# First attention of a two-layer gated block: one quarter of the heads takes its exponential straight from PSUM on ScalarE

## The reference

```python
HEADS = 16; HEAD_DIM = EMBED // HEADS; EXP_DIM = 2 * HEAD_DIM
def _feature_map(x, fm_w, fm_b):
    z = jnp.einsum('nshd,ed->nshe', x, fm_w) + fm_b
    return jnp.concatenate([jnp.exp(z), jnp.exp(-z)], axis=-1)
v, k, q = (_feature_map(x, fm_w, fm_b) for x in (v, k, q))
scores = jnp.einsum('nqhd,nkhd->nhqk', q, k) / jnp.sqrt(jnp.float32(EMBED))
attn = jax.nn.softmax(scores, axis=-1)
out = jnp.einsum('nhql,nlhd->nqhd', attn, v)
return out.reshape(N, S, HEADS * EXP_DIM) @ fc_w.T + fc_b
```

## Time and profile before

| what | value |
|---|---|
| median of 3 runs | 2163.36 us (2162.54 to 2164.04) |
| the profiled execution | 2158.57 us, of it 2156.8 us span |
| TensorE busy | 2027.2 us (94%) |
| VectorE busy | 1896.5 us (88%) |
| ScalarE busy | 1579.3 us (73%) |
| GpSimd busy | 1571.2 us (73%) |

### The profile page before, as it was taken

How to read it: one execution, slowest core, us unless ns; L and a number is a source line. 1 busy time by engine, 2 the same in 40 slices (tenths; PEclk the granted TensorE clock), 3 DMA queues, 4 the chain that set the end, 5 groups by cost and what they waited for, 6 DMA issues and landing times. The chain is left out here.

```text
span 2156.8 us, 82951 instructions
## 1 busy us (share of the span) xinstructions
PE 2027.2 (94%) x28378; PEld 1574.6 (73%) x28380; DVE 1896.5 (88%) x4324; ACT 1579.3 (73%) x3515; POOL 1571.2 (73%) x1456
## 2 busy tenths in 40 slices
PE   3999999977999999999999699999999966999999
PEld 2788888854666666666666689999999954777776
DVE  6899999987888888888888689999999968888888
ACT  3788888866555555655565678888888856888887
POOL 1576777742666666666666789999999943888888
PEclk9999999987999999999999899999999988999999
DMA  5100000002422223222221355555555530000000
GB/s 172 24 6 6 6 7 6 7 2 59 112 84 88 78 82 89 80 79 89 81 78 34 60 82 83 91 83 91 83 90 84 82 73 1 15 10 15 10 15 15
DMA packets 476587, 121.41 MB, mean 56 GB/s; under 512 B 431895, under 2 KB 446871, under 8 KB 475876
## 3 DMA queue, kind: packets, MB, share of 16 engines
q1 hardware_dynamic: 475140, 120.38, 25.4%
q10 hardware_dynamic: 1376, 0.10, 0.0%
HBM read 106.51 MB, written 13.89 MB: 56 GB/s over the span
## 5 line engine op out<-in xcount | busy, mean ns | idle before, releaser
L1286 POOL TENSOR_TENSOR f_low<-f_hidden,f_high 128x512 f16<-128x512 f32 x336 | 442.5, 1322 | 218.2 <-ACT f_high L1218 216.3
L1244 DVE TENSOR_TENSOR f_hidden<-f_hidden,f_share 128x512 f32<-128x512 f32 x336 | 372.8, 1110 | 0.0
L1434 POOL TENSOR_TENSOR f_low<-f_hidden,f_high 128x512 f16<-128x512 f32 x256 | 296.4, 1159 | 68.3 <-ACT f_high L1377 65.2
L1224 ACT ACTIVATE f_act_out<-f_gate 128x512 f32<-128x512 f32 x336 | 200.4, 596 | 193.3 <-PE f_gate L1188 193.1
L1267 DVE SCALAR_TENSOR_TENSOR f_hidden<-f_up,f_act_out 128x512 f32<-128x512 f32 x336 | 229.7, 684 | 82.5 <-PE f_up L1188 52.3
L1218 ACT ACTIVATE f_high<-f_hidden 128x512 f16<-128x512 f32 x336 | 210.5, 627 | 73.3 <-DVE f_hidden L1244 72.0
L1198 PE MATMUL f_y<-w_high,f_high 128*128 128x128 f16 x1344 | 243.5, 220 | 2.0 <-POOL f_low L1286 1.9
L1198 PE MATMUL f_y<-w_low,f_high 128*128 128x128 f16 x1344 | 243.5, 220 | 0.0
L1198 PE MATMUL f_y<-w_high,f_low 128*128 128x128 f16 x1344 | 243.5, 220 | 0.0
L1830 POOL TENSOR_TENSOR a_q_head_high<-a_q_t_high,a_head_mask 128x2048 f16<-128x2048 f16 x64 | 233.0, 3640 | 3.9 <-DVE a_q_t_low L1880 3.2
L1830 POOL TENSOR_TENSOR a_q_head_low<-a_q_t_low,a_head_mask 128x2048 f16<-128x2048 f16 x64 | 233.0, 3641 | 0.0
(11 more groups left out here) (278 smaller groups left out, 8164.5 us busy)
## 6 DMA issues: line engine op xcount, KB each, us to landing
f_share<-expert_shares SPq DMA_DIRECT2D x128, 256.0 KB, 3.2
a_q_pos<-queries SPq DMA_DIRECT2D x64, 512.0 KB
f_share<-expert_shares SPq DMA_DIRECT2D x128, 128.0 KB, 3.0
relative_values<-a_rel_all SPq DMA_DIRECT2D x508, 8.0 KB
f_share<-expert_shares SPq DMA_DIRECT2D x128, 32.0 KB, 1.8
queries<-a_q_parts SPq DMA_DIRECT2D x64, 64.0 KB, 3.2
a_rel<-relative_values SPq DMA_DIRECT2D x64, 64.0 KB, 2.1
out_x<-x_all SPq DMA_DIRECT2D x16, 256.0 KB, 2.0
```

The costliest lines, as they stand in the source:

```text
L1224: nc.scalar.activation(act_out[m % RING][:, :], gate_ps[m % BANKS][:, :], ACT.Silu, scale=1.0 / WSCALE).then_inc(act_ready, 1)
L1244: nc.vector.tensor_tensor(hidden[r][:, :], hidden[r][:, :], share[k][:, :, :].rearrange("p t q -> p (t q)"), ALU.mult).then_inc(scaled, 1)
L1286: nc.gpsimd.tensor_tensor(low[r][:, :], hidden[r][:, :], high[r][:, :], ALU.subtract).then_inc(low_ready, 1)
L1434: nc.gpsimd.tensor_tensor(low[k][:, :], hidden[k][:, :], high[k][:, :], ALU.subtract).then_inc(low_ready, 1)
```

## The change

For quarter 3 of each batch, `subtract_max` on VectorE is dropped. In its place VectorE writes -SCALE times the maxima, 128x4, into a new small tile `bias` (`negate_max`), and ScalarE takes the exponential straight from the scores in `score_ps[1]`, with that bias and the scale SCALE. A bias operand holds one number for each partition, so each of the four heads needs an operation of its own, of 128x77 (`exp_of_scores`). It stands where exp(n-1, 3) stood in ScalarE's list. Since ScalarE now reads `score_ps[1]`, `scores(n, p, 0)` also waits until `exped` has counted all four quarters of batch n - 1; `shifted` now counts three a batch.

```diff
+        negated, bias = sem("negated"), sb("bias", [P, 4])
 ...
                 def scores(n, p, c):
                     if inside(n, 0, B):
                         pe.wait_ge(kfeat_ready, 2 * n + c + 1)
-                        wait(pe, shifted, 4 * n + 2 * c)
+                        wait(pe, shifted, 3 * n + 2 * c)
+                        if c == 0:
+                            wait(pe, exped, 4 * n)
 ...
                 def exp(n, u):
                     if inside(n, 0, B):
-                        act.wait_ge(shifted, 4 * n + u + 1)
+                        act.wait_ge(shifted, 3 * n + u + 1)
                         nc.scalar.activation(prob[u][:, :, :], prob[u][:, :, :], ACT.Exp, scale=SCALE).then_inc(exped, 1)
+
+                def exp_of_scores(n):
+                    if inside(n, 0, B):
+                        act.wait_ge(negated, n + 1)
+                        wait(act, prob_ready, 4 * n)
+                        for j in range(4):
+                            last = nc.scalar.activation(prob[3][:, j, :], score_ps[1][:, KC * j:KC * (j + 1)], ACT.Exp,
+                                                        bias=bias[:, j:j + 1], scale=SCALE)
+                        last.then_inc(exped, 1)
 ...
                 def slot(n, p):
                     o = 1 - p
-                    exp(n - 1, 3)
+                    exp_of_scores(n - 1)
 ...
+                def negate_max(n):
+                    if inside(n, 0, B):
+                        dve.wait_ge(top_ready, 4 * n + 4)
+                        wait(dve, exped, 4 * n)
+                        nc.vector.tensor_scalar(bias[:, :], top[3][:, :], -SCALE, None, ALU.mult).then_inc(negated, 1)
 ...
                     subtract_max(n, 2)
-                    subtract_max(n, 3)
+                    negate_max(n)
```

## The result

The changed kernel takes 2311.3 us (median of 4 runs, 2309.7 to 2312.9) against 2162.95 for the kernel before: a ratio of 1.0684 (95% interval 1.0671 to 1.0698), 148 us slower. I had forecast slower, with 2251 us and a range that ended at 2282. The sign and the stall were right; the time lies outside the range.

A forecast was written before the change was run, and what follows sets the result against it. The prediction took TensorE to bound the first attention at 6.42 us a slot; 61 stalls of 1.43 us plus 0.5 us gave 87.7 us, added to 2163.4 for 2251 us (4.1% slower), range 2235 to 2282.

The forecast's parts named there:

- The sign: Whole kernel: slower, with a chance of 0.95; faster had 0.03.
- the stall: First attention, TensorE before `scores(n+1, 0)`: start at 257.37 in place of 255.94, 1.43 us later in each slot.
- TensorE sets the slot, VectorE's relief is worth nothing: First attention: TensorE streams without a real stop, 6.42 us a slot; unloading VectorE, with 0.20 us of slack, gains nothing.
- the rival in which VectorE was the bound: First attention: VectorE's list sets the pace, the new wait is hidden, 12 us saved, 2151 us; chance 0.04.
- the five terms: Slot's closed loop: 5.89 us of TensorE, then 0.61 + 0.35 + 0.94 + 0.05 us of ScalarE, 7.84 us in all.
- the sum: First attention: 61 slots x 1.43 us, plus 0.5 us at the end, 87.7 us added.
- Hidden under the first DMA wait: Start of the first attention: stalls of slots 1 and 2 vanish in TensorE's 10.91 us wait for batch 3's context.
- The clock: First attention: rival in which TensorE's clock falls because it stands still each slot, 2291 to 2384 us; chance 0.07.
- the same formula: TensorE's 5.89 us a slot lengthened by a lower clock: at 0.9, 0.65 us more in each of 61 slots.
- The small operation on VectorE: `negate_max`, 128x4 from SBUF: between nothing and 0.244 us, taken as 0.2 us.
- neither costs anything: VectorE's `negate_max`: bias ready by 255.2, before ScalarE comes at 256.38, and its wait for the earlier exponential ended; no cost.

The follow-up runs named there:

- Experiment 7: Kernel before, with four extra fp32 128x128 matmuls on TensorE ahead of a batch's first scores and no new wait: 2221.25 us (1.0298).
- experiment 8: Kernel before, with VectorE's subtraction for quarter 3 cut from 308 to 4 columns, that quarter's probabilities left out: 2157.16 us (0.9998).
- Experiment 1: Changed kernel, with four extra fp32 128x128 matmuls on TensorE ahead of the new wait, their results overwritten: 2247.45 us (1.0414).
- Experiment 2: Kernel before, with only one more wait: a batch's first scores also wait for the last exponential of the batch before: 2242.78 us (1.0392).
- experiment 3: Kernel before, with the last quarter's exponential as four 128x77 operations in SBUF, no bias and no new wait: 2158.42 us (1.0001).
- experiment 4: Changed kernel, reordered: last quarter's exponentials earlier in ScalarE's list, TensorE's first scores after two small groups of transposes: 2217.37 us (1.0272).
- 6: Kernel of experiment 4, with quarter 3's maxima written to PSUM so that the operation making the bias reads PSUM: 2185.88 us (1.0135).

## Why the prediction was right, and where it went wrong

**TensorE sets the slot, VectorE's relief is worth nothing.** Right. Experiment 7 shows it from one side, experiment 8 from the other, and the rival in which VectorE was the bound is excluded.

**The stall.** Right in place and size. `scores(n+1, 0)` waits for the last of four exponentials, which take 0.94 us as priced from the key copy of the second attention. Slots without a loss of clock last 7.85 us against a forecast of 7.84, and this is not luck, as each of the five terms came out within 0.01 us. Experiment 1, the stall with the clock held up, took 89 us more than the kernel before; the sum was 87.7. Experiment 2 shows that it is the wait, and experiment 3 that it isn't the number of operations.

**Hidden under the first DMA wait.** The stalls of slots 1 and 2 were to vanish there. The wait for the context of batch 3 shrank from 10.91 to 5.23 us, and TensorE started again at 57.88 against 57.80; they did.

```profile
57.88 1.71 PE L266 MATMUL a_prep<-a_xc,a_fm_w 128*128 128x205 f32 x4 [5.23 <-DMA a_xc<-in_ctx]
```

**The clock.** This is the step that failed. I had made it a rival with a chance of 0.07 and wrote that "the new share would be 6.4 of 7.84, or 82%" against a stretch of 79% that had kept 1.00. So the sum took the cost of the clock as nothing and the forecast said that it stays at 1.00; it measured 0.88 and 58 us, which is nearly all of the 60 us between the forecast of 2251 and the 2311. The mechanism was described rightly in the rival and its size fairly: 2291 at a mean clock of 0.9. By the same formula 0.88 is 5.89 / 0.88 - 5.89 = 0.80 us a slot, 49 us, where the slots lost 58. Its chance was wrong, because the comparison was. The stretch that kept its clock is 10 us of other matmuls in the second attention, and its idle time lies at its two ends, with none between (a view of the kernel before):

```profile
1728.64 0.20 PE L1623 MATMUL a_score<-a_k_t_high,a_q_head_high 128*128 128x77 f16 x1 [1.05 <-DMA a_q_pos<-queries]
1738.81 0.20 PE L1623 MATMUL a_score<-a_k_t_high,a_q_head_high 128*128 128x77 f16 x1 [2.23 <-DMA a_q_pos<-queries]
```

Here an idle time of 1.36 us comes in every slot, some 60 times, and the one stretch with a low clock that I had, 30 us at 0.73, I argued away. The runs show what the views of before couldn't: an idle time of 1.36 us a slot gave 0.88, 0.95 us gave 0.94, and the same stalls with TensorE's idle time cut to 0.8 or 0.4 us by useless work gave 1.00. The Trainium skill, page TensorE: Matmul & The Clock Gate, section A second HAM failure mode: psum-queue depth-cycling, says that frequent short idle times can make the clock swing between its levels; that is what the changed kernel's trace shows, slot by slot, and I should have given it a far larger chance.

What stays open is why one slot loses its clock and the next, with the same idle time, doesn't, and whether it is the length of the single idle time that counts or TensorE's idle time in all: in these runs the two rose and fell together.

**The small operation on VectorE.** I took 0.2 us, bounded by 0.244, from a row of another operation, and it took 0.157 to 1.052 us. The step "neither costs anything" held for the change, since VectorE had time to spare. It failed as soon as experiment 4 took that time away.

## What to carry to other kernels

When an engine is to read a buffer that the bound engine will overwrite, ask first where that read stands in its queue: here one wait behind four operations cost 86 us, while four operations in place of one, without the wait, cost nothing. Once TensorE gets a recurring idle time, price the clock as a likely second cost and not a remote one: here it added 58 us to 86, and useless matmuls in the gap restored the clock. Unloading an engine that is 97% busy is worth nothing if another one, with no slack, sets the pace; a few extra operations on the suspected bound, and a few fewer on the other engine, show which it is.

## What the runs showed of the hardware

TensorE's clock fell for about 3 us at a time, to a granted 0.50, in 35 of 60 slots in each of which it was idle once for 1.36 us, and in 14 of 60 with 0.95 us; in no slot with 0.8 or 0.4 us. Eight transposes took 1.92 us at the low level and 1.04 us at the high one.

A VectorE operation of 128x4 from SBUF to SBUF took 1.09 us, ending when GpSimd's masking ended, and 0.15 us when its source was in PSUM. The Trainium skill, page SBUF — State Buffer, section Who interferes with whom, says that VectorE's `tensor_scalar` can, in some of its modes, take the port pair that it shares with GpSimd, and that whichever of the two comes second is then blocked until the other's instruction is over, and that outside such modes an operation with at most one input from SBUF doesn't contend. Experiments 4 and 6 agree, with 1.09 and 0.15 us, but experiment 4 goes further: VectorE's operation began during the first of two maskings and ended only with the second. Why it waited for the second too is not shown.
